# A fused language-model block on one core: two more units of each attention step are written ahead, and SyncE's queue is reordered

## The chip, the cores and the metric

The kernel runs on one core of a Trainium2 chip. The metric is the device time of one execution in microseconds (us). Engines are called PE (TensorE, the matmuls), DVE (VectorE), ACT (ScalarE), POOL (GpSimd) and SP (SyncE, which here only issues DMA transfers).

## What is computed

An embedding with a short grouped convolution and ReLU, then attention with a residual, then a block with layer norms and eight experts chosen by position, all in float32 on 2 sequences of 1024 tokens with 128 channels. The change touches the attention, whose core in the reference is

```python
q, k, v = (proj(Wq), proj(Wk), proj(Wv))          # 8 heads of 64
dots = jnp.einsum('bhqd,bhkd->bhqk', q, k) * scale
attn = jax.nn.softmax(dots, axis=-1)
out = jnp.einsum('bhqk,bhkd->bhqd', attn, v)
out = jnp.einsum('bne,ce->bnc', out, Wo)
```

and at its edges the first layer norms of the block behind it.

## The kernel before

**Steps, units, parts.** There are 8 attention steps (STEPS), one for each sequence and pair of heads. A step has 16 units (s, kc, half): 128 keys (kc 0 to 7) against 512 queries (half 0 or 1) for two heads. A unit is scores on PE into a pair of PSUM banks, exponentials on ACT out of it, and the values' product on PE. Units run in 8 parts of two, half 0 in parts 0 to 3 and half 1 in parts 4 to 7.

**Maxima.** The softmax needs each query's maximum ahead of the exponentials. It is taken from a product of its own ("max" items, matmuls of L576, two heads each), which DVE reduces (L1066), and which runs ahead of the units: 14 items stand in front of step 0 (AHEAD), then two in each part. So the 8 items of half 0 of step s+1 end in part 4 of step s, those of half 1 in part 0 of step s+1. When a half is complete, DVE joins it (L1074), and SP does the rest (max_rows, L426): 8 column transfers bring the maxima from partitions into rows (L438), one stores the rows in HBM (L443), one loads them back spread over 128 partitions as a plane (L448). SP waits between these for each to land.

**Written ahead or not.** A unit in FILLED gets its PSUM banks filled with minus the plane before its scores are added: by ACT alone (fill, L903), or, in HALVED, one head by DVE (fill_half, L1110, a "share") and one by ACT (L901). A unit that is UNFILLED instead gets a fourth pair of matmuls from minus_rows and max_rows_of (in scores, L623 to L638), which needs only the rows. 30 of the 128 units are unfilled: the first two of every step among them (LATE_PLANES), because their banks would have to be filled in the last part of the step before.

**Order.** part_items and beside_values write one list for all engines, and each engine runs its own part of it strictly in order: a waiting instruction holds up all behind it on its engine. k and q of step s+1 are computed in part 0 of step s. Units use banks 0 to 3 (EVEN_PAIR, ODD_PAIR), and "max" items take two each from a ring of three banks (RING), so that each shares a bank with the one before it and must wait until that one's first head has been reduced (holders, release).

**Reciprocals.** The softmax sums of step s-1 go through SP in step s (spread, L412): a transfer to a flat layout, a reciprocal on DVE in part 4, a store to HBM (L417), and two loads of 256 KB that spread it (L422), after which POOL multiplies (normalise, L1293). SP's order in a step is: rows of (s, 1), all of spread, rows of (s+1, 0), in steps 4 to 6 two experts' weights (L454).

**Step 7** has no more k, q and, after part 0, no maxima; instead the first sequence's output product (wo, 64 matmuls of L585), its layer norms on ACT ("norms") and two products for the block behind it (nt, xa) run among its units.

Of the kernel before, what the change touches and what calls it, by code (L numbers as in the profile page):

```python
# [51 lines left out]
AHEAD = 14  # L52
# [75 lines left out]
NO_SLOT = ("join", "hidden", "pv", "o", "inv", "norms", "fill", "share")  # L128
# [26 lines left out]
def step_pairs(items):  # L155

    pairs, turn = [], 0
    for item in items:
        if item[0] == "exp":
            pairs.append(ODD_PAIR if item[2] % 2 else EVEN_PAIR)  # L160
        elif item[0] in ("k", "wo"):
# [45 lines left out]
def build(nc, x, tables, w_in, wo_in, small_in, next_b, fc_in, out):  # L207
    VOCAB = VOCAB_ROWS
    with ExitStack() as ctx:
# [136 lines left out]
        rows_stored, plane_loaded, filled_in, half_filled = (sem(n) for n in ("rows_stored", "plane_loaded", "filled_in", "half_filled"))  # L346
# [57 lines left out]
        def _(sp):  # L404
# [7 lines left out]
            def spread(s):  # L412
# [4 lines left out]
                sp.dma_start(inv_dram[:, :], inv_flat[:, :]).then_inc(inv_stored, 16)  # L417
                sp.wait_ge(inv_stored, s * 16 + 16)
# [7 lines left out]
            def max_rows(v, half):  # L426
# [6 lines left out]
                for c in range(GROUP):  # L433
                    qc = half * GROUP + c
                    if i == 0:
                        sp.wait_ge(max_joined, c + 1)
                    for h in range(2):
                        sp.dma_start(max_rows_of[v % 2][h * D:h * D + 1, qc * CHUNK:(qc + 1) * CHUNK].bitcast(F32),  # L438
                                     maxes[:, h, qc:qc + 1].bitcast(F32)).then_inc(rows_loaded, 16)
                sp.wait_ge(rows_loaded, ROW_COUNT * (i + 1))  # L440
# [4 lines left out]
                if i > 1:  # L445
                    sp.wait_ge(filled_in, filled_up_to(i - 2, FILLED))
                    sp.wait_ge(half_filled, filled_up_to(i - 2, HALVED))
# [37 lines left out]
        def _(pe):  # L485
# [241 lines left out]
            for s in range(STEPS):  # L727
                for item, n in numbered(STEP_ITEMS[s], FIRST[s]):
# [7 lines left out]
                    if item[0] == "exp" and item[1:] in FILLED:  # L736
                        pe.wait_ge(filled_in, FILLED.index(item[1:]) + 1)
                        if item[1:] in HALVED:
                            pe.wait_ge(half_filled, HALVED.index(item[1:]) + 1)
# [46 lines left out]
        def _(act):  # L786
# [80 lines left out]
            def early_norms(which, dst, done):  # L867

                for j in range(KCH):
# [22 lines left out]
            def fill(unit_item):  # L892
# [7 lines left out]
                if unit_item[1:] in HALVED:  # L900
                    act.activation(to[:, 1, :], plane[:, 1, :], ACT.Copy, scale=-1.0).then_inc(filled_in, 1)  # L901
                else:
                    act.activation(to, plane, ACT.Copy, scale=-1.0).then_inc(filled_in, 1)  # L903
# [18 lines left out]
            for s in range(STEPS):  # L922
                for item, n in numbered(STEP_ITEMS[s], FIRST[s]):
                    if item[0] in ("fill", "share") and item[1:] in FILLED:
# [3 lines left out]
                    elif item == ("norms", 1):  # L928
                        ln_sqrt(0)
                    elif item == ("norms", 2):  # L930
                        act.wait_ge(shifted, 2)
                        early_norms(1, normed2, n2_made)
                    elif item == ("norms", 3):
                        early_norms(0, h1n, n1_made)
# [48 lines left out]
        def _(dve):  # L983
# [119 lines left out]
            def fill_half(unit_item):  # L1103
# [48 lines left out]
            def dve_step(s):  # L1152
                for item, n in numbered(STEP_ITEMS[s], FIRST[s]):
                    if item[0] == "inv":
                        invert(item[1])
                    elif item[0] == "share" and item[1:] in HALVED:
                        fill_half(item)
                    elif item[0] == "join":
                        join_last_pair()
                    elif item == ("norms", 1):  # L1160
# [197 lines left out]
```

## Time and profile before

| what | value |
|---|---|
| median of 3 executions | 402.34 us (402.18 to 472.35) |
| the profiled execution | 404.02 us, of which span 402.2 us |
| PE busy | 386.5 us (96%), 2378 matmuls |
| POOL busy | 292.9 us (73%) |
| ACT busy | 290.1 us (72%) |
| DVE busy | 261.8 us (65%) |
| mean granted TensorE clock | 0.996 |
| matmuls from minus_rows | 60 |

The span runs from the first to the last instruction. Start and duration in a timeline are in us from its start. The attention steps take most of it, from about 40 to 352 us; in front are embedding, convolution, norms and projections, behind it the experts. A busy PE isn't PE at its peak: matmuls are pipelined, so the distance between starts tells more than the durations.

### The profile page before, as it was taken

What the parts mean: (1) busy time and instruction counts of PE and PEld (TensorE: products, weight loads), DVE (VectorE), ACT (ScalarE), POOL (GpSimd) and SP (SyncE); (2) the same over time, 40 slices, a digit from 0 to 9 for tenths busy, and PEclk for the clock granted to TensorE, in tenths of its full rate; (3) what the DMA queues carried; (4) which work ended last, traced back from release to release, by engine and by line L of the source; (5) the groups of instructions that cost most, each with busy time, mean ns of one, the idle gap of its engine ahead of it and who ended that gap; (6) DMA issues with size and microseconds to landing.
All of it is one profiled execution on the core that took longest, in us unless ns stands there. A gap on an engine that the chain in (4) does not pass through costs nothing.

```text
span 402.2 us, 6740 instructions
## 1 busy us (share of the span) xinstructions
PE 386.5 (96%) x2378; PEld 221.6 (55%) x2378; DVE 261.8 (65%) x470; ACT 290.1 (72%) x402; POOL 292.9 (73%) x145
## 2 busy tenths in 40 slices
PE   8988899999999999999999999999999887999996
PEld 8754644554464446444544544454457434489995
DVE  6998677676867776766778687767773401664322
ACT  3665489778968886887889688968861897636763
POOL 3170099969899999989998999999897676900021
PEclk9999899999999999999999999999999999999999
DMA  4001010101222022112012420251034105000001
GB/s 141 8 0 53 0 55 0 54 3 52 57 53 54 4 53 54 54 41 66 2 55 55 133 75 4 55 157 56 22 69 125 53 1 155 4 2 15 13 28 52
DMA packets 28229, 19.45 MB, mean 48 GB/s; under 512 B 21249, under 2 KB 23681, under 8 KB 28197
## 3 DMA queue, kind: packets, MB, share of 16 engines
q1 hardware_dynamic: 27620, 18.05, 16.8%
q10 hardware_dynamic: 576, 0.98, 0.8%
q8 instruction: 19, 0.31, 0.4%
q14 instruction: 14, 0.11, 0.1%
HBM read 17.72 MB, written 1.17 MB: 47 GB/s over the span
## 4 chain that ended last, share of the span: by engine, by line
PE 75%; ACT 14%; issue 5%; DVE 4%; ACTq 0%; DVEq 0%
PE psum L649 22%; PE psum L638 20%; ACT probs L834 8%; PE psum L576 8%; PE psum L564 5%; PE psum L585 4%; PE psum L706 4%; PE psum L695 4%; PE psum L540 2%; ACT psum L903 2%; PE psum L660 1%; ACT attn_out L911 1%; PE psum L515 1%; DVE half_maxes L1062 1%; PE psum L601 1%
## 5 line engine op out<-in xcount | busy, mean ns | idle before, releaser
L1066 DVE TENSOR_REDUCE half_maxes<-psum 128x1 f32<-128x512 f32 x228 | 146.5, 684 | 38.1 <-PE psum L576 37.8
L834 ACT ACTIVATE probs<-psum 128x1024 f32<-128x1024 f32 x128 | 128.6, 1018 | 40.7 <-PE psum L638 39.6
L649 PE MATMUL psum<-probs,v_all 128*64 128x512 f32 x512 | 123.7, 604 | 0.0
L1282 POOL TENSOR_TENSOR sums<-sums,probs 128x1024 f32<-128x1024 f32 x31 | 74.2, 2393 | 2.6 <-ACT probs L834 2.5
L1282 POOL TENSOR_TENSOR odd_sum<-odd_sum,probs 128x1024 f32<-128x1024 f32 x31 | 74.4, 2399 | 0.0
L1282 POOL TENSOR_TENSOR sums<-probs 128x1024 f32<-128x1024 f32 x16 | 38.0, 2376 | 44.1 <-ACT probs L834 44.0
L649 PEld LDWEIGHTS psum<-probs,v_all 128*64 128x64 f32 x512 | 31.2, 136 | 62.2 <-issue 47.5
L1110 DVE TENSOR_SCALAR psum<-max_plane 128x512 f32<-128x512 f32 x46 | 32.0, 695 | 45.0 <-ACT probs L834 45.0
L638 PE MATMUL psum<-q_round,k_round 64*128 64x512 f32 x256 | 55.2, 426 | 5.3 <-ACT psum L903 2.0
L576 PE MATMUL psum<-k_round,q_round 64*128 64x512 f32 x256 | 56.5, 445 | 3.1 <-DVE half_maxes L1062 1.5
L903 ACT ACTIVATE psum<-max_plane 128x1024 f32<-128x1024 f32 x52 | 53.6, 1030 | 4.5
L576 PEld LDWEIGHTS psum<-k_round,q_round 64*128 64x128 f32 x256 | 24.0, 185 | 53.5 <-DVE half_maxes L1066 34.9
L638 PE MATMUL psum<-q_round,k_rest 64*128 64x512 f32 x256 | 51.2, 393 | 0.0
L638 PE MATMUL psum<-q_rest,k_round 64*128 64x512 f32 x256 | 51.0, 392 | 0.0
L1288 POOL TENSOR_TENSOR sums<-sums,odd_sum 128x1024 f32<-128x1024 f32 x16 | 38.1, 2382 | 1.3
L638 PEld LDWEIGHTS psum<-q_round,k_round 64*128 64x128 f32 x256 | 24.4, 185 | 26.1 <-ACT psum L903 14.5
L1282 POOL TENSOR_TENSOR odd_sum<-probs 128x1024 f32<-128x1024 f32 x16 | 38.3, 2395 | 0.0
L1310 POOL TENSOR_TENSOR probs<-probs,residual 128x256 f32<-128x256 f32 x7 | 5.1, 726 | 42.7 <-ACT probs L954 42.7
L901 ACT ACTIVATE psum<-max_plane 128x512 f32<-128x512 f32 x46 | 27.7, 602 | 5.2
L638 PEld LDWEIGHTS psum<-q_round,k_rest 64*128 64x128 f32 x256 | 24.5, 185 | 5.5
L638 PEld LDWEIGHTS psum<-q_rest,k_round 64*128 64x128 f32 x256 | 24.5, 186 | 3.2
L947 ACT ACTIVATE probs<-psum,small 128x128 f32<-128x128 f32 x64 | 17.4, 383 | 11.4 <-PE psum L695 11.4
(123 smaller groups left out, 456.4 us busy)
## 6 DMA issues: line engine op xcount, KB each, us to landing
max_plane<-rows_scratch SPq DMA_DIRECT2D x16, 512.0 KB, 3.7
inv_sb<-inv_scratch SPq DMA_DIRECT2D x14, 256.0 KB, 3.9
max_rows_of<-maxes SPq DMA_DIRECT2D x128, 0.5 KB, 2.0
v_all<-in_fc SPq DMA_DIRECT2D x4, 512.0 KB, 5.7
fc_late<-in_fc SPq DMA_DIRECT2D x4, 512.0 KB, 5.8
out_h<-probs SPq DMA_DIRECT2D x8, 128.0 KB, 1.8
v_all<-in_w ACTq DMA_DIRECT2D x3, 256.0 KB, 3.6
woT<-in_wo SPq DMA_DIRECT2D x1, 256.0 KB, 3.5
```

Of the source, the lines that this page charges most:

```text
L564: last = pe.matmul(slot[:, half, :], ws[:, w, v % PAIRS, :], xs[:, cols[half]], start=(i == 0), stop=(i == 2))
L576: last = pe.matmul(slot[:, h, :], q_round[p][head_rows(h), qc * CHUNK:(qc + 1) * CHUNK], k_round[p][head_rows(h), half * BANK:(half + 1) * ...
L638: last = pe.matmul(slot[:, h, :], stationary, qs[head_rows(h), cols], start=(i == 0 and not ahead), stop=(i == len(terms) - 1), skip_group ...
L649: last = pe.matmul(out_bank[head_rows(h), :], v_all[:, s, kc, head_rows(h)], probs[unit(s, kc, half) % TILES][:, h, :], start=(kc == 0), s ...
L834: last = act.activation(probs[u % TILES][:, heads, :], source, ACT.Exp, scale=SCALE)
L901: act.activation(to[:, 1, :], plane[:, 1, :], ACT.Copy, scale=-1.0).then_inc(filled_in, 1)
L903: act.activation(to, plane, ACT.Copy, scale=-1.0).then_inc(filled_in, 1)
L947: act.activation(hidT[d % 2][:, i, r, :], slot[:, i, r], ACT.Gelu, bias=fc1_b_col[:, e * HC + r:e * HC + r + 1]).then_inc(hid_made, 1)
L1066: dve.reduce_max(half_maxes[:, h, qc, keys:keys + 1], slot[:, h, :], AX.X).then_inc(maxed, 1)
L1110: dve.tensor_scalar(pair_view(PAIRS_OF[n])[:, 0, :], plane[:, 0, :], -1.0, None, ALU.mult).then_inc(half_filled, 1)
L1282: pool.tensor_tensor(chain[:, :, :], first[:, :, :], probs[kc][:, :, :], ALU.add).then_inc(own, 1)
L1288: pool.tensor_tensor(even[:, :, :], even[:, :, :], odd_sum[:, :, :], ALU.add).then_inc(own, 1)
```

## The change

- AHEAD goes from 14 to 12; the first five parts of step 0 take 1, 2, 3, 3 and 3 maxima (FIRST_COUNTS), after which the count is what it was. k and q of step 1 move from part 0 to part 1.
- The first two units of steps 1 to 7 are now written ahead, in the last part of the step before (following looks across the step's end): the first shared by DVE and ACT, the second by ACT. In step 0 six units more are unfilled. In all 18 units are unfilled.
- In step 7 twelve units are written wholly by DVE (VECTOR_FILLED); wo moves to the end of part 0 and from the units' banks to the ring; nt moves from part 3 to part 4, xa from 5 to 6, and the norms are cut into four groups of four.
- On SP the former spread and max_rows are cut in two each, and in a step the columns of (s+1, 0) go out in front of the reciprocals' loads.

```diff
-AHEAD = 14
+AHEAD = 12
...
-FFN_ITEMS = {(STEPS - 1, 0): [("wo",)], (STEPS - 1, 3): [("nt",)], (STEPS - 1, 5): [("xa",)], (STEPS - 1, 6): [("last den", 0)]}
-
-
-LATE_PLANES = [(s, kc, 0) for s in range(STEPS) for kc in (0, 1)]
-BEHIND_K, BEHIND_Q = [(s, 2, 0) for s in range(STEPS)], [(s, 3, 0) for s in range(STEPS)]
-UNFILLED = LATE_PLANES + BEHIND_Q + [(0, 2, 0), (STEPS - 1, 2, 0), (STEPS - 1, 4, 0), (STEPS - 1, 5, 0), (STEPS - 1, 0, 1), (STEPS - 1, 1, 1)]
+FFN_ITEMS = {(STEPS - 1, 4): [("nt",)], (STEPS - 1, 6): [("xa",), ("last den", 0)]}
+LAST_NORMS = {1: [("roots",)], 2: [("n2", 0)], 3: [("n2", 1)], 4: [("n1", 0)], 5: [("n1", 1)]}
+
+
+FIRST_UNITS = [(0, kc, 0) for kc in (0, 1)]
+BEHIND_K = [(0, 4, 0)] + [(s, 2, 0) for s in range(1, STEPS - 1)]
+BEHIND_Q = [(0, 5, 0)] + [(s, 3, 0) for s in range(1, STEPS - 1)]
+FIRST_PLANES = [(0, kc, 0) for kc in (2, 3, 6)] + [(0, kc, 1) for kc in (0, 1, 2, 3)]
+UNFILLED = FIRST_UNITS + BEHIND_Q + FIRST_PLANES + [(STEPS - 1, 4, 0), (STEPS - 1, 5, 0)]
...
-HALVED = [u for u in FILLED if u[1] % 2 == 0 and u not in BEHIND_K]
+BESIDE_LAST_MAXES = [(STEPS - 1, kc, 0) for kc in (0, 1)]
+SCALAR_FILLED = [u for u in FILLED if u[0] < STEPS - 1 or u in BESIDE_LAST_MAXES]
+HALVED = [u for u in SCALAR_FILLED if u[1] % 2 == 0 and u not in BEHIND_K]
+VECTOR_FILLED = [u for u in FILLED if u in HALVED or u not in SCALAR_FILLED]
...
-    if part == 0 and s + 1 < STEPS:
+    if part == (0 if s > 0 else 1) and s + 1 < STEPS:
         items += [("k", s + 1), ("q", s + 1)]
...
+FIRST_COUNTS = (1, 2, 3, 3, 3)
+
+
+def maxes_before(turn):
+
+    return AHEAD + sum(FIRST_COUNTS[:turn]) + 2 * max(0, turn - len(FIRST_COUNTS))
+
+
 def part_items(s, part):
 
-    maxes = [("max", *m) for m in MAXES[AHEAD + 2 * (s * PARTS + part):][:2]]
-    items = maxes[:1]
+    turn = s * PARTS + part
+    maxes = [("max", *m) for m in MAXES[maxes_before(turn):maxes_before(turn + 1)]]
     first, second = [("exp", *u) for u in units_of(s, part)]
-    following = units_of(s, part + 1) if part + 1 < PARTS else []
-    items += [first] + [("share", *u) for u in following if u in HALVED] + [second] + maxes[1:]
-    beside = beside_values(s, part)
-    items += beside
-    items += [("fill", *u) for u in following if u in FILLED and u not in HALVED]
-    if s > 0 or part > 0:
-        items += [("pv", *u) for u in units_of(*divmod(s * PARTS + part - 1, PARTS))]
+    following = units_of(*divmod(turn + 1, PARTS)) if turn + 1 < STEPS * PARTS else []
+    shares = [[("share", *u)] * (u in VECTOR_FILLED) for u in following] or [[], []]
+    if turn == 0:
+        items = [first, second] + maxes
+    elif len(maxes) == 3:
+        items = [maxes[0], first] + shares[0] + [maxes[1], second] + shares[1] + maxes[2:]
+    elif (s, part) == (STEPS - 1, 0):
+        items = maxes[:1] + [first, second] + maxes[1:] + shares[0] + shares[1]
+    else:
+        items = maxes[:1] + [first] + shares[0] + [second] + shares[1] + maxes[1:]
+    items += beside_values(s, part)
+    items += [("fill", *u) for u in following if u in SCALAR_FILLED]
+    if turn > 0:
+        items += [("pv", *u) for u in units_of(*divmod(turn - 1, PARTS))]
     if part == 0 and s > 0:
         items.append(("o", s - 1, 1))
     if part == 4:
         items += [("o", s, 0)] + [("inv", s - 1)] * (s > 0)
-    if s == STEPS - 1 and part in (1, 2, 3):
-        items.append(("norms", part))
+    if s == STEPS - 1:
+        items += [("wo",)] * (part == 0) + LAST_NORMS.get(part, [])
     return items
...
-            max_rows(0, 0)
+            load_rows(0, 0)
+            spread_rows(0, 0)
             early, late = list(EARLY_EXPERTS), list(LATE_EXPERTS)
             for s in range(STEPS):
-                max_rows(s, 1)
+                load_rows(s, 1)
+                spread_rows(s, 1)
                 if s > 0:
-                    spread(s - 1)
+                    store_inverse(s - 1)
                 if s + 1 < STEPS:
-                    max_rows(s + 1, 0)
+                    load_rows(s + 1, 0)
+                if s > 0:
+                    spread_inverse(s - 1)
+                if s + 1 < STEPS:
+                    spread_rows(s + 1, 0)
...
-            def fill_half(unit_item):
+            def vector_fill(unit_item):
 
                 _, s, kc, half = unit_item
                 n = ALL_ITEMS.index(("exp", s, kc, half))
-                plane = max_planes[half][:, :].rearrange("p (h n) -> p h n", h=2)
+                to, plane = pair_view(PAIRS_OF[n]), max_planes[half][:, :].rearrange("p (h n) -> p h n", h=2)
                 dve.wait_ge(*release(ALL_ITEMS[holders(n)[0][0]]))
                 dve.wait_ge(plane_loaded, 16 * (2 * s + half) + 16)
-                dve.tensor_scalar(pair_view(PAIRS_OF[n])[:, 0, :], plane[:, 0, :], -1.0, None, ALU.mult).then_inc(half_filled, 1)
+                heads = slice(0, 1 if unit_item[1:] in HALVED else 2)
+                dve.tensor_scalar(to[:, heads, :], plane[:, heads, :], -1.0, None, ALU.mult).then_inc(vector_filled, 1)
```

load_rows is max_rows up to its column transfers, spread_rows the rest of it (from the wait for them, L443 on); store_inverse is spread up to the store of the reciprocals, spread_inverse the rest of it, with the two loads.

## Rows read from the trace of the kernel before

**Rows 1.** Stretches: us, then busy us of each engine, clock, DMA share, GB/s

```profile
core 0: us, PE busy (x) PEld busy (x) DVE busy (x) ACT busy (x) POOL busy (x), PEclk, DMA share, GB/s
151.00:188.00 37.00, 36.87 (x222) 17.81 (x218) 27.01 (x43) 29.84 (x34) 35.29 (x16) 1.00 0.18 44
```

**Rows 2.** Timeline of PE, into step 4: start, duration, what

```profile
186.31 0.40 PE L576 MATMUL psum<-k_round,q_round 64*128 64x512 f32 x2
...
188.51 0.50 PE L576 MATMUL psum<-k_round,q_round 64*128 64x512 f32 x2
...
189.54 0.39 PE L638 MATMUL psum<-max_rows_of,minus_rows 64*128 64x512 f32 x2
189.76 0.39 PE L638 MATMUL psum<-q_round,k_round 64*128 64x512 f32 x2
```

**Rows 3.** Timeline of ACT, same transition; in brackets the idle time before

```profile
185.82 1.94 ACT L834 ACTIVATE probs<-psum 128x1024 f32<-128x1024 f32 x2 [0.40 <-PE psum L638]
189.97 1.96 ACT L834 ACTIVATE probs<-psum 128x1024 f32<-128x1024 f32 x2 [2.21 <-PE psum L638]
```

**Rows 4.** Timeline of DVE, same transition

```profile
176.45 0.17 DVE L1074 TENSOR_REDUCE maxes<-half_maxes 128x8 fp32r<-128x16 f32 x1
...
186.75 1.29 DVE L1066 TENSOR_REDUCE half_maxes<-psum 128x1 f32<-128x512 f32 x2 [0.33 <-PE psum L576]
```

**Rows 5.** Timeline of SP's queue, same transition: when a DMA is issued

```profile
176.81 0.32 SPq L417 DMA_DIRECT2D inv_scratch<-inv_flat  x1
178.21 1.15 SPq L422 DMA_DIRECT2D inv_sb<-inv_scratch  x2
179.45 5.04 SPq L438 DMA_DIRECT2D max_rows_of<-maxes  x8
185.93 0.53 SPq L443 DMA_DIRECT2D rows_scratch<-max_rows_of  x1
187.54 0.32 SPq L448 DMA_DIRECT2D max_plane<-rows_scratch  x1
```

**Rows 6.** Issue to landing: inv_sb's two (178 to 180), first column (179.4 to 180), plane (187 to 189)

```profile
DMA to landing us min/median/max: 3.6/3.9/4.1
...
max_rows_of<-maxes SPq DMA_DIRECT2D x1, 0.5 KB, 3.4
...
max_plane<-rows_scratch SPq DMA_DIRECT2D x1, 512.0 KB, 3.6
```

**Rows 7.** Groups by line, DVE's share: count, then busy, mean ns, idle before

```profile
L1110 DVE TENSOR_SCALAR psum<-max_plane 128x512 f32<-128x512 f32 x46 | 32.0, 695 | 45.0 <-ACT probs L834 45.0
```

**Rows 8.** Issue to landing, plane with experts' loads behind it, 262.2 to 263

```profile
max_plane<-rows_scratch SPq DMA_DIRECT2D x1, 512.0 KB, 4.4
```

**Rows 9.** Timeline of POOL, same transition

```profile
188.17 2.40 POOL L1293 TENSOR_TENSOR attn_out<-attn_out,inv_sb 128x1024 f32<-128x1024 f32 x1
```

**Rows 10.** Stretches around PE's clock, columns as in rows 1

```profile
38.00:41.00 3.00, 1.39 (x12) 0.85 (x10) 3.00 (x3) 0.00 (x0) 0.00 (x0) 1.00 0.46 175
41.00:44.50 3.50, 3.50 (x17) 2.27 (x14) 2.01 (x4) 1.86 (x2) 0.00 (x0) 0.51 0.00 0
332.00:336.00 4.00, 1.71 (x12) 0.72 (x10) 0.85 (x2) 3.77 (x6) 1.74 (x1) 1.00 0.02 2
```

**Rows 11.** PE's waits from 37 to 51 us: in total, times, longest

```profile
PE psum L576 <- ACT q_round L845: 1.2, 1, 1.2
PE psum L576 <- DVE half_maxes L1062: 1.0, 1, 1.0
PE psum L638 <- DVE half_maxes L1062: 0.6, 1, 0.6
```

**Rows 12.** PE's waits from 300 to 352 us

```profile
PE psum L638 <- ACT psum L903: 2.0, 2, 1.0
PE psum L638 <- DVE psum L1110: 1.6, 2, 1.3
PE psum L592 <- ACT normed L870: 1.2, 1, 1.2
PE psum L638 <- DVE residual L1125: 0.8, 1, 0.8
```

More of the change, by code:

```diff
@@ L125, in step_items @@
     return items
-NO_SLOT = ("join", "hidden", "pv", "o", "inv", "norms", "fill", "share")
+NO_SLOT = ("join", "hidden", "pv", "o", "inv", "roots", "n1", "n2", "fill", "share")
 def numbered(items, first):
@@ L160, in step_pairs @@
             pairs.append(ODD_PAIR if item[2] % 2 else EVEN_PAIR)
-        elif item[0] in ("k", "wo"):
+        elif item[0] == "k":
             pairs.append(EVEN_PAIR)
@@ L345, in build @@
         rows_loaded = sem("rows_loaded")
-        rows_stored, plane_loaded, filled_in, half_filled = (sem(n) for n in ("rows_stored", "plane_loaded", "filled_in", "half_filled"))
+        rows_stored, plane_loaded, scalar_filled, vector_filled = (sem(n) for n in ("rows_stored", "plane_loaded", "scalar_filled", "vector_filled"))
         summed = [[sem(f"summed_{p}_{half}") for half in ("low", "high")] for p in ("even", "odd")]
@@ L410, in _, with store_inverse @@
             sp.dma_start(woT[:, :, :], wo_in).then_inc(wo_loaded, 16)
-            def spread(s):
+            def store_inverse(s):
                 sp.wait_ge(den_copied, s + 1)
@@ L417, in spread, with spread_inverse @@
                 sp.dma_start(inv_dram[:, :], inv_flat[:, :]).then_inc(inv_stored, 16)
+            def spread_inverse(s):
                 sp.wait_ge(inv_stored, s * 16 + 16)
@@ L424, in spread, with load_rows @@
                                  .partition_broadcast(D).rearrange("p a n -> p (a n)")).then_inc(inv_loaded, 16)
-            def max_rows(v, half):
+            def load_rows(v, half):
                 i = 2 * v + half
@@ L439, in max_rows, with spread_rows @@
                                      maxes[:, h, qc:qc + 1].bitcast(F32)).then_inc(rows_loaded, 16)
+            def spread_rows(v, half):
+                i = 2 * v + half
                 sp.wait_ge(rows_loaded, ROW_COUNT * (i + 1))
@@ L445, in max_rows @@
                 if i > 1:
-                    sp.wait_ge(filled_in, filled_up_to(i - 2, FILLED))
-                    sp.wait_ge(half_filled, filled_up_to(i - 2, HALVED))
+                    sp.wait_ge(scalar_filled, filled_up_to(i - 2, SCALAR_FILLED))
+                    sp.wait_ge(vector_filled, filled_up_to(i - 2, VECTOR_FILLED))
                 sp.dma_start(max_planes[half][:, :], rows_dram[half:half + 1].rearrange("a h n -> a (h n)").partition_broadcast(128)
@@ L736, in _ @@
                     if item[0] == "exp" and item[1:] in FILLED:
-                        pe.wait_ge(filled_in, FILLED.index(item[1:]) + 1)
-                        if item[1:] in HALVED:
-                            pe.wait_ge(half_filled, HALVED.index(item[1:]) + 1)
+                        if item[1:] in SCALAR_FILLED:
+                            pe.wait_ge(scalar_filled, SCALAR_FILLED.index(item[1:]) + 1)
+                        if item[1:] in VECTOR_FILLED:
+                            pe.wait_ge(vector_filled, VECTOR_FILLED.index(item[1:]) + 1)
                     else:
@@ L865, in ln_sqrt, with early_norms @@
                                bias=eps_squared[:, 0:1]).then_inc(ln_std, 1)
-            def early_norms(which, dst, done):
-                for j in range(KCH):
+            def early_norms(which, half, dst, done):
+                if (which, half) == (1, 0):
+                    act.wait_ge(shifted, 2)
+                for j in range(half * GROUP, (half + 1) * GROUP):
                     act.activation(dst[:, j, :], residual[:, j, :], ACT.Identity, bias=shift[:, which, j:j + 1],
@@ L900, in fill @@
                 if unit_item[1:] in HALVED:
-                    act.activation(to[:, 1, :], plane[:, 1, :], ACT.Copy, scale=-1.0).then_inc(filled_in, 1)
+                    act.activation(to[:, 1, :], plane[:, 1, :], ACT.Copy, scale=-1.0).then_inc(scalar_filled, 1)
                 else:
-                    act.activation(to, plane, ACT.Copy, scale=-1.0).then_inc(filled_in, 1)
+                    act.activation(to, plane, ACT.Copy, scale=-1.0).then_inc(scalar_filled, 1)
             def o_copy(s, half):
@@ L923, in _ @@
                 for item, n in numbered(STEP_ITEMS[s], FIRST[s]):
-                    if item[0] in ("fill", "share") and item[1:] in FILLED:
+                    if item[0] == "fill":
                         fill(item)
@@ L927, in _ @@
                         o_copy(item[1], item[2])
-                    elif item == ("norms", 1):
+                    elif item[0] == "roots":
                         ln_sqrt(0)
[L930 to L934, printed above, removed]
+                    elif item[0] == "n2":
+                        early_norms(1, item[1], normed2, n2_made)
+                    elif item[0] == "n1":
+                        early_norms(0, item[1], h1n, n1_made)
                     if n is not None:
@@ L1155, in dve_step @@
                         invert(item[1])
-                    elif item[0] == "share" and item[1:] in HALVED:
-                        fill_half(item)
+                    elif item[0] == "share":
+                        vector_fill(item)
                     elif item[0] == "join":
                         join_last_pair()
-                    elif item == ("norms", 1):
+                    elif item[0] == "roots":
                         ln_inverse(0)
```

## The prediction

> **What bounds the kernel now.** I read the page's list of engines first, then the table of stretches, then the timelines of one transition between two attention steps, engine by engine, SP's queue last. In a step of 37.0 us TensorE (PE) is busy 36.87 us and shows a granted clock of 1.00, GpSimd 35.29, ScalarE 29.84, VectorE 27.01 [rows 1]. So PE sets the pace, and any time in which PE has nothing to do is lost whole: nothing else stands ahead of it. GpSimd's 35.3 us would be the next floor, far enough off for the sizes below. The thing to see in PE's timeline is that part 7 of a step and part 0 of the next run on without a gap: max product at 186.31, then the values' products, then the next max product at 188.51 [rows 2].
>
> **The change, part by part.**
>
> *Products saved on PE.* A unit that isn't written ahead needs one more pair of matmuls (minus_rows). The pair starts at 189.54 and the next one at 189.76 [rows 2]: about 0.23 us a pair with the neighbours' spacing. Before, 30 of 128 units have it; after, 18: the two first units of steps 1 to 7 are gained (14), four more in step 7 too, and six of step 0 are given up: 14 + 4 - 6 = 12. Sum: -12 x 0.23 = **-2.8 us**, about 0.46 us for each transition.
>
> *What writes them instead.* In part 7 ScalarE writes 1.5 units and VectorE half a unit more. Counted as work this costs nothing: ScalarE is idle 2.21 us before the exponentials at 189.97 [rows 3] and VectorE has 10 us spare in a step [rows 1]. But these instructions wait, and what matters is for what.
>
> *When the plane of maxima is there.* These are the times of the transition into step 4. The last half maximum of the half is joined at 176.45 + 0.17 = 176.62 [rows 4]. SP issues the reciprocals' store at 176.81, their two loads at 178.21, the eight columns from 179.45 to 184.49, the rows' store at 185.93 (1.44 after the last issue) and the plane at 187.54 (1.61 later) [rows 5]. The plane lands 3.6 us later, 191.1 [rows 6]. With the columns in front, they are issued from about 177.2 to 182.25 and the reciprocals' loads from 182.3 to 183.5. The last column has landed at 183.7, and the rows' store goes out then. From here there are two ends:
> - nothing in its way: plane issued 183.7 + 1.6 = 185.3, landed **188.9**;
> - the store stands in the queue behind the two loads of 256 KB. Rows 6 show such a case: the first column, issued at 179.45 right behind those loads, took 3.4 us (landed 182.85) and not the 2.0 or so of one with nothing ahead (0.63 of issue plus 1.44). The second load, issued about 178.8, lands 3.6 to 4.1 later, so at 182.4 to 182.9: the small transfer came when the large one had. In the new order the second load goes out at 182.9 and lands 186.5 to 187.0; the store with it; the plane then lands at **190.1 to 190.6**.
>
> I take the second. The Trainium skill (DMA: Bandwidth & Descriptors, section Queues, rings and completion order) says that an engine takes descriptors in ring order but that a later one may finish its write first; the 3.4 us agree with its first half, and by its second half alone the sum would be that of the first end.
>
> *Who waits.* VectorE's share of unit (s+1, 0, 0) stands in part 7 behind the first exponential, which starts at 185.82 and has ended by about 186.9 [rows 3]. The plane is 2 us late at the one end and 3.2 to 3.7 at the other. VectorE runs in program order, so the reductions of part 7's second max product, done at 186.75 before [rows 4], now stand behind that share. The next max product of PE (188.51) shares a bank with that product and waits until its first head is reduced. After the plane: a share of 0.695 [rows 7], a first reduction of 0.65 (half of 1.29 [rows 4]), some 0.1 between engines: 1.45 us. PE resumes at 190.35 at the one end, at 191.55 to 192.05 at the other, instead of 188.51. PE waits **1.8** or **3.0 to 3.5 us**; I take 3.3. Behind it stand the scores, k and q of the next step and all values' products. Six transitions (into steps 2 to 7) have reciprocals: 6 x 3.3 = **+19.8 us**. Into steps 5, 6 and 7 the experts' loads are issued right behind the plane, and such a plane took 4.4 us, not 3.6 [rows 8]: 3 x 0.8 = **+2.4 us**. Into step 1 there are no reciprocals, and parts 4 and 5 of step 0 have no units that VectorE writes ahead while PE has two more pairs in each; I take 0, with 1.2 us (the 1.8 less about 0.55 for the reciprocals' store) as the bound above.
>
> *What waits for the reciprocals.* Their loads land at about 187.0, 4 us later than before. GpSimd normalises at 188.17 [rows 9]: hidden by 1.1 us, and PE's wait adds to that. If it weren't, GpSimd would wait, and only after that the exponentials.
>
> *The clock.* From 38 to 41 us PE was busy 1.39 of 3.0 us, and from 41.0 to 44.5 its clock was granted at 0.51, the 1.2 GHz level instead of 2.4. A stretch with 1.71 of 4.0 busy (332 to 336) was not followed by a drop [rows 10]. A single wait of 3.3 us is longer than any there. I take one such slow stretch for each of the six: 3.4 us at half speed lose 1.7: 6 x 1.7 = **+10.2 us**; the bound below is 0. The Trainium skill (TensorE: Matmul & The Clock Gate, Part 1) has the clock fall with low activity and return with work, which these rows agree with.
>
> *Start.* AHEAD = 12 takes two maxima off the front, and k and q of step 1 go into part 1. PE's waits of 1.0 and 0.6 us before the first exponential and of 1.2 us on q_round [rows 11] go, since PE then has exponentials and values' products to run, and the slow stretch of rows 10 (1.7 us) should go with them: 1.0 + 0.6 + 1.2 + 1.7 = **-4.5 us**. Three maxima a part are 3 x 1.29 of reductions plus at most one share, about what PE needs for such a part; bound: nothing gained.
>
> *Step 7.* PE waits 2.0 + 1.6 + 1.2 + 0.8 = 5.6 us there [rows 12]. The 0.8 (units waiting for the wo bank) goes; VectorE writes 12 whole units (up to 1.39 us each, twice 0.695), ScalarE loses that work, and its 16 norms come in fours. But roots and both table loads still stand between exponentials while PE has no more than two units of lead. I take **-1.0 us**, bounds -4 and +2.
>
> *Sum.* -2.8 + 19.8 + 2.4 + 10.2 - 4.5 - 1.0 = +24.1. The profiled execution took 404.0 us (span 402.2), the median is 402.34, its span's size; on it: **426 us**, 6% slower.
>
> **The rivals.**
> - *The clock holds.* All as above, without the +10.2: 416 us. For it: no drop after 332 to 336. Against it: there PE worked between two short waits.
> - *The store isn't held by the loads.* The wait is 1.8, not 3.3: 9 us less. If the clock holds as well: 402.3 - 2.8 + 10.8 + 2.4 - 4.5 - 1.0 = 407 us; if it drops, 417. For it: the store is 4 KB and needs only its own rings; against it: the 3.4 us of rows 6.
> - *The plane is in time* (the other side). The columns go 2.25 us earlier, and if the rest of the chain closes up so that the plane lands before the share asks for it (186.9), no wait arises: 402.3 - 2.8 - 4.5 - 1.0 = 394 us. This decides from a landing 4.2 us before today's 191.1; the lead of the columns is 2.25. Between 186.9 and there every us late is a us of PE in each of six steps; break-even is a wait of about 0.9 us, a landing near 188.
> - *Nearly no change.* The landing is somewhat earlier than my lower end, or the gains at the start and in step 7 reach their bounds: 396 to 409 us.
>
> **How the numbers follow.** Forecast (queue holds the store, clock drops: 420 to 434): 0.50. Clock holds (411 to 420): 0.22. Store not held: 0.15, half near 407, half near 417. In time: 0.06. Nearly no change: 0.07. The likeliest gives 426. A measurement of this kernel tells about 2% from no change: below 394.3 faster (0.06), above 410.4 slower (0.50 + 0.22 + 0.07 = 0.79), between them same (0.08 + 0.07 = 0.15). The range reaches from the store not held with the clock holding, 407, rounded to 408, to 433, the forecast with waits of 3.7 us and a smaller gain at the start; about 0.2 lies outside.
>
> **What would show it.** In the new profile: 18 x 2 matmuls from minus_rows instead of 60. In SP's timeline the columns' issue ahead of the reciprocals' loads, and the gap from the last column's issue to the plane's issue growing from 3.05 us to about 4.7 (queue holds) or staying (not). On PE six waits of about 3.3 us on half_maxes, once a step, in front of part 0's max product, with VectorE idle before its share until a DMA lands. A clock below 1.00 once behind each. Wrong would be: no such waits, or a plane landed by the end of part 7's first exponential; waits of half the size with the gap unchanged, the second rival; waits in place with a clock of 1.00, the first. Waits of the step-7 kind instead would say that the fills, not the plane, are late.

## The result

| | before | after |
|---|---|---|
| median | 402.31 us | 430.18 us (429.15 to 431.09) |
| ratio | | 1.069, 95% interval 1.066 to 1.072 |
| span of the profiled execution | 402.2 us | 429.3 us |
| mean granted clock | 0.996 | 0.964 |
| matmuls from minus_rows | 60 | 36 |

One execution of before took 472 us, and the ratio leaves it out. The change made the kernel 6.9% slower; 426 us was forecast.

PE's waits by what ended them (in total, times, longest) in the kernel after:

```profile
PE psum L610 <- DVE half_maxes L1102: 31.1, 9, 5.6
PE psum L672 <- DVE psum L1147: 2.2, 4, 1.0
```

Of the 31.1 us, seven waits stand at the start of a step: 1.33, 5.26, 3.69, 3.73, 4.79, 5.62 and 5.60 into steps 1 to 7, 30.0 together. Before there was no such wait: PE went on at 188.51 without idle time [rows 2]. The transition into step 4 in the kernel after, SP's queue first (start, duration of the issue):

```profile
185.97 0.32 SPq L438 DMA_DIRECT2D inv_scratch<-inv_flat  x1
186.39 5.01 SPq L462 DMA_DIRECT2D max_rows_of<-maxes  x8
191.49 1.19 SPq L446 DMA_DIRECT2D inv_sb<-inv_scratch  x2
192.86 0.52 SPq L471 DMA_DIRECT2D rows_scratch<-max_rows_of  x1
195.88 0.32 SPq L476 DMA_DIRECT2D max_plane<-rows_scratch  x1
```

The columns are out at 191.40 and landed by 192.86, but from the rows' store to the plane's issue it takes 3.02 us, against 1.61 before [rows 5]: the store came back late, behind the reciprocals' two loads. The plane then took this long from issue to landing:

```profile
DMA to landing us min/median/max: 3.5/3.5/3.5
```

So it landed at 199.4. DVE's timeline (in brackets the idle time and what ended it):

```profile
193.69 1.29 DVE L1102 TENSOR_REDUCE half_maxes<-psum 128x1 f32<-128x512 f32 x2 [0.28 <-PE psum L610]
199.42 0.69 DVE L1147 TENSOR_SCALAR psum<-max_plane 128x512 f32<-128x512 f32 x1 [4.45 <-DMA max_plane<-rows_scratch]
200.03 2.65 DVE L1102 TENSOR_REDUCE half_maxes<-psum 128x1 f32<-128x512 f32 x4
```

DVE stands idle 4.45 us before its share, and the two reductions of a max product that PE had started at 194.87 begin only at 200.03, where before they ran at 186.75, right behind their product [rows 4]. PE's timeline ends the chain:

```profile
195.18 1.94 PE L683 MATMUL psum<-probs,v_all 128*64 128x512 f32 x8
200.85 0.50 PE L610 MATMUL psum<-k_round,q_round 64*128 64x512 f32 x2 [3.73 <-DVE half_maxes L1102]
...
201.96 0.67 PE L672 MATMUL psum<-q_round,k_round 64*128 64x512 f32 x2
202.39 0.67 PE L672 MATMUL psum<-q_rest,k_round 64*128 64x512 f32 x2
```

The second pair of lines is the clock: starts 0.43 us apart and not 0.23. The same stretch in the table of windows (us, PE busy, weight loads, DVE, ACT, POOL, clock, DMA share, GB/s):

```profile
197.00:207.00 10.00, 6.27 (x29) 4.79 (x28) 4.63 (x8) 4.47 (x5) 9.41 (x5) 0.83 0.14 49
```

**Where the 27.1 us between the spans arose.** PE's first product of step 1 stood at 77.27 us before and at 77.08 after: -0.2, although a wait of 1.3 us is in it. From there to the same product of step 7 it took 222.5 us (to 299.74) and now 252.0 (to 329.11): +29.6. Step 7, up to its last sums' product (353.76 and 380.86), took 54.0 and now 51.7: -2.3. The rest, 48.4 us, is the same. -0.2 + 29.6 - 2.3 = 27.1.

### The profile page after: what moved, and what is told of

It is laid out like the page before. It is cut to its first block, busy times and chain, and to the rows that moved or that the text cites. A ratio compares the mean times of both kernels' runs of the same rounds, so it can differ in the third digit from the quotient of the medians.

```text
span 429.3 us, 6704 instructions
## 1 busy us (share of the span) xinstructions
PE 389.0 (91%) x2354; PEld 229.6 (53%) x2354; DVE 274.7 (64%) x483; ACT 284.5 (66%) x402; POOL 292.3 (68%) x145
## 4 chain that ended last, share of the span: by engine, by line
PE 61%; DMA 15%; DVE 9%; SPq 8%; issue 4%; ACT 4%; DVEq 0%
PE psum L683 15%; PE psum L672 14%; SPq L462 7%; PE psum L610 7%; DMA max_plane<-rows_scratch 6%; PE psum L598 5%; DMA rows_scratch<-max_rows_of 5%; DMA max_rows_of<-maxes 4%; PE psum L619 3%; PE psum L740 3%; PE psum L729 3%; DVE half_maxes L1102 3%; ACT probs L869 2%; PE psum L574 2%; DVE psum L1147 2%
## 5 line engine op out<-in xcount | busy, mean ns | idle before, releaser
L1102 DVE TENSOR_REDUCE half_maxes<-psum 128x1 f32<-128x512 f32 x232 | 148.9, 683 | 32.9 <-PE psum L610 31.9
L869 ACT ACTIVATE probs<-psum 128x1024 f32<-128x1024 f32 x128 | 125.3, 1022 | 58.6 <-PE psum L672 58.1
L610 PE MATMUL psum<-k_round,q_round 64*128 64x512 f32 x256 | 59.6, 464 | 32.0 <-DVE half_maxes L1102 31.1
L1147 DVE TENSOR_SCALAR psum<-max_plane 128x512 f32<-128x512 f32 (+1 forms) x57 | 45.4, 806 | 61.5 <-DMA max_plane<-rows_scratch 35.1
L610 PEld LDWEIGHTS psum<-k_round,q_round 64*128 64x128 f32 x256 | 25.7, 193 | 84.3 <-DVE half_maxes L1102 71.7
L672 PE MATMUL psum<-q_round,k_rest 64*128 64x512 f32 x256 | 53.6, 410 | 0.0
L672 PE MATMUL psum<-q_rest,k_round 64*128 64x512 f32 x256 | 53.3, 408 | 0.0
L672 PEld LDWEIGHTS psum<-q_round,k_round 64*128 64x128 f32 x256 | 25.9, 194 | 11.9 <-DVE psum L1147 6.5
L672 PEld LDWEIGHTS psum<-q_round,k_rest 64*128 64x128 f32 x256 | 26.1, 195 | 5.6
L672 PEld LDWEIGHTS psum<-q_rest,k_round 64*128 64x128 f32 x256 | 26.1, 196 | 4.8
```

Source lines behind the costliest of these rows:

```text
L610: last = pe.matmul(slot[:, h, :], q_round[p][head_rows(h), qc * CHUNK:(qc + 1) * CHUNK], k_round[p][head_rows(h), half * BANK:(half + 1) * ...
L672: last = pe.matmul(slot[:, h, :], stationary, qs[head_rows(h), cols], start=(i == 0 and not ahead), stop=(i == len(terms) - 1), skip_group ...
L869: last = act.activation(probs[u % TILES][:, heads, :], source, ACT.Exp, scale=SCALE)
L1102: dve.reduce_max(half_maxes[:, h, qc, keys:keys + 1], slot[:, h, :], AX.X).then_inc(maxed, 1)
L1147: dve.tensor_scalar(to[:, heads, :], plane[:, heads, :], -1.0, None, ALU.mult).then_inc(vector_filled, 1)
```

## The experiments

The theory: the plane of half 0 isn't there when DVE's share of the next step's first unit asks for it, the share holds the reductions behind it, these hold PE, and the clock drops in the wait. The rivals: the fills cost as work, or SP's new order costs by itself.

**First two units unfilled again.**

```diff
-UNFILLED = FIRST_UNITS + BEHIND_Q + FIRST_PLANES + [(STEPS - 1, 4, 0), (STEPS - 1, 5, 0)]
+UNFILLED = FIRST_UNITS + BEHIND_Q + FIRST_PLANES + [(STEPS - 1, 4, 0), (STEPS - 1, 5, 0)] + [(s, kc, 0) for s in range(1, STEPS) for kc in (0, 1)]
```

> The kernel after, but the first two units of steps 1 to 7 are not written ahead again (14 pairs of matmuls from minus_rows more); all else, SP's order too, as after. Theory (the share that waits for the plane costs PE its waits and the clock drops behind them): the seven waits on half_maxes (30.0 us in the profile after) and the slow stretches (about 12.7 us lost) go, 14 x 0.23 = 3.2 us come back: 430.2 - 30.0 - 12.7 + 3.2 = 391 us. Rival (SP's new order or the new order of fills is what costs): stays above 410 us.

Measured: 392.5 us, ratio to before 0.976 (0.974 to 0.977), clock 1.00; of the waits on half_maxes 1.1 us are left. The whole loss hangs on these 14 units. And all the rest of the change is worth 10 us, far more than I had forecast for it. A step took 36.17 us where it had taken 37.04 (from one k_rest on DVE to the next: 152.92 to 189.09, and 156.79 to 193.83 before), with as many unfilled units. That wanted an explanation of its own (below).

**SP's order of before, with the two units written ahead.**

```diff
+                if s > 0:
+                    spread_inverse(s - 1)
                 if s + 1 < STEPS:
                     load_rows(s + 1, 0)
-                if s > 0:
-                    spread_inverse(s - 1)
-                if s + 1 < STEPS:
                     spread_rows(s + 1, 0)
```

> The kernel after, but SP issues the reciprocals' loads ahead of the columns again, as before. From the reciprocals' store to the plane's issue it was 10.73 us before (176.81 to 187.54) and 9.91 after (185.97 to 195.88). Theory (each us by which the plane lands later is a us of PE in each of six transitions): 430.2 + 6 x 0.8 = 435 us, waits of about 4.5 us. Rival (the reorder gave its full 2.25 us of lead): 430.2 + 13 = 443 us. Rival (it gave nothing): 430 us.

Measured: 439.5 us (ratio 1.092), waits on half_maxes 37.5 in all against 31.1. The reorder did help the change, by 9.3 us in the medians and 7.1 in the two profiled executions (spans 436.4 and 429.3). 6.4 of the 7.1 are waits, the rest a little more slow clock (0.957 against 0.964). Of the 6.4, 0.7 lies in the wait into step 1 (2.08 us instead of 1.33), where there are no reciprocals. From part 7's last max product to the next step's first, the six other transitions lost 5.7 us, 0.95 each: near the 0.8 of my theory, and 1.3 short of the columns' whole lead of 2.25. About that much (1.4) the store behind the loads takes back, as the next experiment shows.

**The reciprocals' loads behind the plane.**

```diff
                 if s + 1 < STEPS:
                     load_rows(s + 1, 0)
+                    spread_rows(s + 1, 0)
                 if s > 0:
                     spread_inverse(s - 1)
-                if s + 1 < STEPS:
-                    spread_rows(s + 1, 0)
```

> The kernel after, but the reciprocals' loads are issued behind the plane, so that nothing large stands between the columns and the rows' store. Theory (the store is held in the queue by the two loads: 3.0 us from its issue to the plane's issue after, 1.6 before): the gap returns to 1.6, the reciprocals' two issues (1.2 us) no longer delay it either, the waits fall by about 1.5 us each, six times 9 us: about 421 us, less if the clock then drops less often; the reciprocals come later, at about GpSimd's turn. Rival (the store is slow for another reason): gap stays near 3.0, 430 us.

Measured: 419.9 us, 10.3 less than after (9.6 by the two profiled spans). SP's queue into step 4:

```profile
183.85 5.01 SPq L462 DMA_DIRECT2D max_rows_of<-maxes  x8
190.30 0.53 SPq L471 DMA_DIRECT2D rows_scratch<-max_rows_of  x1
191.91 0.32 SPq L476 DMA_DIRECT2D max_plane<-rows_scratch  x1
192.32 1.15 SPq L446 DMA_DIRECT2D inv_sb<-inv_scratch  x2
```

From store to plane 1.61 us again. A store of 4 KB came back 1.4 us later with 512 KB ahead of it in its queue. Whether their order in the queue did that, or only that they were under way at the same time, the runs don't separate. All waits on half_maxes came to 24.6 us, 6.5 less. GpSimd, whose reciprocals now come later, cost nothing that can be seen.

**Matmuls in the wait.**

```diff
+                        if s > 0 and item == ("max", *MAXES[min(maxes_before(s * PARTS), len(MAXES) - 1)]):
+                            m, k = holders(n)[0]
+                            pe.wait_ge(*release(ALL_ITEMS[m], k))
+                            p, cols = item[1] % 2, slice(item[2] * CHUNK, (item[2] + 1) * CHUNK)
+                            for _ in range(14):
+                                pe.matmul(bank(PAIRS_OF[n][0]), q_round[p][:, cols], k_round[p][:, 0:BANK], start=True, stop=True)
                         for m, k in holders(n):
                             pe.wait_ge(*release(ALL_ITEMS[m], k))
```

> The kernel after, with 14 matmuls of 512 columns (3.0 us) whose result is overwritten put into PE's waits at the start of steps 1 to 7, on a bank that is free by then. Theory (the granted clock falls because PE has nothing to do in the wait, and that loses about 12.7 us beside the waits): clock 1.00 or near, 430.2 - 12.7 = 417.5 us, into step 1 up to 1.7 us longer. Rival (the drop costs nothing, since the others wait for PE anyway or it comes from something else): 430 us.

Measured: 423.3 us, 6.9 less than after. The window that showed 0.83 above:

```profile
197.00:207.00 10.00, 9.15 (x48) 6.38 (x48) 5.78 (x9) 5.33 (x6) 9.12 (x4) 1.00 0.14 48
```

The drop does come from PE's idle time. What it costs is best read on stretches that hold no transition, from a step's first max product to the second one of its part 7. In this kernel they are 33.7 to 33.8 us in all six steps. In after they were 33.71 us in step 1, which has no slow stretch, and 35.65, 34.97, 34.96, 34.93 and 35.60 in steps 2 to 6: 7.3 us more. Step 7, from its first product to its last sums' product, took 49.1 us here and 51.75 in after: 2.65 more. So the six drops cost 10.0 us.

The median fell by less, 6.9 (8.3 between the profiled spans). Into step 1, where the wait had been only 1.3, the matmuls delayed PE by 2.0 us: from part 7's last max product to the next first it took 5.61 us instead of 3.60. My 12.7, half of all slow time in which PE worked, was too much: even at full clock, k's first matmul waits about 0.3 us for an exponential in these places, and a slow PE covers that.

**The fills' order on ScalarE.** The gain of 0.87 us a step wasn't in my prediction. In the diff, ACT handles only "fill" items, and "fill" items now include the shared units; before, ACT wrote its head of a shared unit at the "share" item, between the two exponentials of a part. This is that edit alone, on the kernel before:

```diff
-    items += [("fill", *u) for u in following if u in FILLED and u not in HALVED]
+    items += [("fill", *u) for u in following if u in FILLED]
...
-                    if item[0] in ("fill", "share") and item[1:] in FILLED:
+                    if item[0] == "fill":
```

> The kernel before, with one edit: ScalarE writes its head of a shared unit behind both exponentials of the part, as the kernel after does, not between them. In the first experiment a step took 36.18 us between two k_rest on VectorE, against 37.05 before, with as many unfilled units per step. Theory (ScalarE's fill between the exponentials delayed the second one, and that was the 0.2 to 0.3 us by which parts 3, 5 and 6 were longer): 402.3 - 7 x 0.87 = 396 us. Rival (the shorter step comes from something else, such as where k and q or the reciprocals stand): 402 us.

Measured: 395.5 us, ratio 0.982 (0.979 to 0.984): by itself it makes the kernel before 1.6 to 2.1% faster, clear of the noise. ACT's timeline before, and then in this kernel:

```profile
160.22 1.03 ACT L834 ACTIVATE probs<-psum 128x1024 f32<-128x1024 f32 x1 [0.54 <-PE psum L638]
161.36 0.60 ACT L901 ACTIVATE psum<-max_plane 128x512 f32<-128x512 f32 x1
161.89 1.00 ACT L834 ACTIVATE probs<-psum 128x1024 f32<-128x1024 f32 x1
163.01 1.03 ACT L903 ACTIVATE psum<-max_plane 128x1024 f32<-128x1024 f32 x1
```

```profile
160.08 1.94 ACT L834 ACTIVATE probs<-psum 128x1024 f32<-128x1024 f32 x2 [0.77 <-PE psum L638]
161.90 0.61 ACT L901 ACTIVATE psum<-max_plane 128x512 f32<-128x512 f32 x1
162.42 1.03 ACT L903 ACTIVATE psum<-max_plane 128x1024 f32<-128x1024 f32 x1
163.99 1.94 ACT L834 ACTIVATE probs<-psum 128x1024 f32<-128x1024 f32 x2 [0.54 <-PE psum L638]
```

Two exponentials at a stretch take 1.94 us; with a fill between them it was 2.67 from the first start to the second end (160.22 to 162.89). ACT still comes round in time: it even idles 0.54 before the next part. PE's weight loads show what had waited. Over two steps (118.33 to 192.46 us), before and then in this kernel:

```profile
PEld psum L638 <- ACT psum L903: 3.4, 10, 0.5
```

```profile
PEld psum L638 <- ACT psum L903: 0.3, 2, 0.2
```

With the second exponential late, ACT's whole fill (L903) behind it was late too, and the next scores' weight loads waited for it: 3.1 us less in two steps, and the two steps became 1.7 us shorter.

**First experiment with SP's old order.** The edit of the second experiment on the first one.

> The first experiment (after, first two units unfilled) with SP's order of before. Theory (the queue's order matters only through the plane, and without the two units the plane has more than 4 us of room): same as the first experiment, 392.5 us. Rival (the reorder helps or harms on its own, by later reciprocals or collisions): more than 1 us off it.

Measured: 392.2 us, ratio 0.973 (0.971 to 0.975), the same. The queue's order is worth nothing where nobody asks for the plane in part 7. Of the kernels that leave nothing out this is the fastest, with the first experiment beside it.

**Share behind both reductions.**

```diff
+    elif part == PARTS - 1:
+        items = maxes[:1] + [first, second] + maxes[1:] + shares[0] + shares[1]
     else:
         items = maxes[:1] + [first] + shares[0] + [second] + shares[1] + maxes[1:]
```

> The kernel after, but in part 7 VectorE takes its share of the next step's first unit behind both reductions. Theory (PE's next max product waits for a reduction that is queued behind the share): that product runs at once, and PE waits for the plane plus a share (0.8) before the scores and not for the plane plus share plus half a reduction (1.45) before the max product (0.34): 1.0 us less a transition, seven times: 430.2 - 7 = 423 us; the wait on PE is then on psum L1147 or L940 and not on half_maxes. Rival (the order on VectorE doesn't matter, ScalarE's fills behind the plane are what PE waits for): 430 us.

Measured: 422.5 us. The wait moved to where the theory put it:

```profile
PE psum L674 <- ACT psum L940: 22.8, 7, 4.8
```

Seven waits for ScalarE's fill, 22.8 us, instead of 30.0 us in seven on half_maxes. The order on DVE was a part of the cost, 1 us a transition; the late plane is the rest.

**Maxima one part earlier.** Meant to bring the plane in time:

```diff
-FIRST_COUNTS = (1, 2, 3, 3, 3)
+COUNTS = [1, 2, 3, 3, 3, 2, 2, 2] + [2, 3, 3, 2, 2, 2, 2, 2] + [0, 3, 3, 2, 2, 2, 2, 2] * 5
...
-    return AHEAD + sum(FIRST_COUNTS[:turn]) + 2 * max(0, turn - len(FIRST_COUNTS))
+    return AHEAD + sum(COUNTS[:turn])
...
+                if s + 1 < STEPS:
+                    load_rows(s + 1, 0)
+                    spread_rows(s + 1, 0)
                 if s > 0:
                     store_inverse(s - 1)
-                if s + 1 < STEPS:
-                    load_rows(s + 1, 0)
-                if s > 0:
                     spread_inverse(s - 1)
-                if s + 1 < STEPS:
-                    spread_rows(s + 1, 0)
```

> The kernel after, but from step 1 on the maxima of half 0 are complete at the end of part 3 and not in part 4 (0, 3, 3, 2, 2, 2, 2, 2 a part), and SP handles rows and plane of (s+1, 0) whole ahead of the reciprocals. Theory (the two units gain their 0.46 us a step once the plane is there in time): join to landing 11.7 us against 13.6 from the end of part 3 to the share: no waits into steps 2 to 7, clock 1.00, against the first experiment 14 x 0.23 = 3.2 us less, 1.3 us of wait into step 1 and up to 2 us for two parts of three reductions a step: 390 to 392 us. Rival (the units written ahead cost in their own right, by ScalarE's and VectorE's work): above 396 us.

Measured: 463.5 us (ratio 1.152). A miss by my own edit. Two of its waits:

```profile
DVE inv_flat L1150 <- DMA den_flat<-den_sb: 39.7, 6, 7.1
PE psum L608 <- DVE half_maxes L1100: 53.1, 27, 6.4
```

store_inverse also holds the flat transfer of the sums, and behind the plane's chain it came 6 to 7 us after DVE's reciprocal in part 4 had begun to wait for it: the change's own fault once more, a DVE instruction in front of the reductions that waits for a late transfer. Besides, each part with three maxima made PE wait 1.0 to 1.1 us, over 2 us a step for a gain below 0.5, so that the form as such couldn't pay. It doesn't tell what an early plane is worth. A mended form was not tried.

**The two units from a plane that is there.** In fill and vector_fill:

```diff
-                act.wait_ge(plane_loaded, 16 * (2 * s + half) + 16)
-                to, plane = pair_view(PAIRS_OF[n]), max_planes[half][:, :].rearrange("p (h n) -> p h n", h=2)
+                early = half == 0 and kc < 2 and s > 0
+                act.wait_ge(plane_loaded, 16 * (2 * s + half) + 16 * (not early))
+                to, plane = pair_view(PAIRS_OF[n]), max_planes[1 if early else half][:, :].rearrange("p (h n) -> p h n", h=2)
```

and on SP the load of the next plane of half 1 waits for these reads too.

> The kernel after, but the first two units of steps 1 to 7 are filled from the plane that is already there, that of the step before's half 1, instead of their own. It leaves out the right maxima for these units (the numbers of the output change, the work doesn't): same instructions, same transfers, only nobody waits for the late plane. Theory (the two units are worth their 14 x 0.23 = 3.2 us, and all of the loss is the wait and the clock behind it): the first experiment's 392.5 - 3.2 = 389.3 us, clock 1.00. Rival (ScalarE's and VectorE's work for the two units costs by itself): 392 us or more.

Measured: 390.4 us, clock 1.00. With the same instructions and transfers and no wait, the kernel is 40 us faster than after. The two profiled spans differ by 40.8 us, and the waits and the clock close that: from part 7's last max product to the next first it takes 30.5 us less in the seven transitions, the slow stretches of after cost 9.9 us, and 0.4 arose before part 7 of step 0 ended. Against the first experiment (392.5) the 14 units gain 2.1 us, not 3.2: a step takes 35.95 us, 0.22 less. The pair costs PE 0.23 each, but k's first matmul then waits for the second exponential:

```profile
PE psum L599 <- ACT probs L870: 1.8, 6, 0.3
```

**Both means against the wait.** Share behind the reductions as above, and on SP:

```diff
                 if s > 0:
-                    store_inverse(s - 1)
+                    flatten(s - 1)
                 if s + 1 < STEPS:
                     load_rows(s + 1, 0)
+                    spread_rows(s + 1, 0)
                 if s > 0:
+                    store_inverse(s - 1)
                     spread_inverse(s - 1)
-                if s + 1 < STEPS:
-                    spread_rows(s + 1, 0)
```

where flatten is the flat transfer of the sums alone.

> The kernel after with both means against the wait: on SP only the flat transfer of the sums stays ahead, then columns, store and plane, and the reciprocals' store and loads behind them; on VectorE the share behind both reductions. With the plane ahead of the loads the six waits were 3.0 to 4.5 (mean 3.6), the share behind the reductions took 1.0 off, the reciprocals' store out of the way takes 0.55 (0.42 of issue and the wait for the reciprocal): mean 2.1 us. Theory (each us of wait is a us of the kernel, on the 389.3 us of an early plane): 389.3 + 6 x 2.1 + 0.7 = 403 us if the clock holds, up to 1.4 a transition more if it drops: 411 us. It stays above the first experiment's 392.5 in any case. Rival (the waits overlap with the rest once they are short): near 390 us.

Measured: 405.0 us (401.4 to 406.8), ratio 1.005 (1.002 to 1.008). In the profiled execution (span 402.3) the waits were 10.1 us in seven:

```profile
PE psum L677 <- ACT psum L943: 10.1, 7, 2.5
```

They were 1.0 us into step 1, then 2.2, 0.9, 0.7, 1.3, 1.6 and 2.5: 1.5 in the mean of the six, shorter than my 2.1. The clock fell once, behind the 2.2 us into step 2:

```profile
116.00:119.40 3.40, 3.40 (x16) 2.21 (x14) 1.61 (x4) 2.26 (x3) 0.00 (x0) 0.52 0.64 154
```

Together with 388.5 us, the span of the kernel with the stale plane, 388.5 + 10.1 = 398.6. Of the other 3.7 us, about 1.2 is that slow stretch, and nearly 0.3 more than its wait stands in each of the seven transitions. The execution with the clock at 1.000 took 401.4 us; in the nine others it was 0.985 to 0.996, and they took 404.1 to 406.8. So the order of SP and DVE brings the change back to the time of before, and leaves it 13 us behind the first experiment. What an early plane with the right maxima gives was never measured.

## Why the prediction was right, and where it was off

- **The mechanism** held in every link: columns early, store held, plane late, share in front of the reductions, PE waiting, clock falling. The kernels with the loads behind the plane, the share behind the reductions, the matmuls in the wait and the stale plane show the links one by one.
- **When the plane is there.** From the last column's issue to the plane's 4.7 us were foreseen and 4.5 came. The end with the store held by the loads was the right one, as rows 6 had said; the Trainium skill (DMA: Bandwidth & Descriptors, section Queues, rings and completion order) has it that an engine takes descriptors in ring order, and the 3.02 and 1.61 us agree with that.
- **The waits, 19.8 + 2.4 = 22.2 us, were mis-sized: 30.0.** Where nothing else came in, 3.3 was near (3.69 and 3.73). The three with experts' loads behind the plane took 4.8 to 5.6, not 4.1, and the one into step 2 took 5.3: there the two loads' issue lasted 2.48 us on SP, not 1.18. I had taken one transition's queue for all. Into step 1, the wait was near the bound I gave (1.2) and not 0. And part of it is demand: with ACT's new order parts 5 to 7 are faster, so PE arrives about 0.55 us earlier (11.15 us from the reciprocals' store to the wait, 11.70 before).
- **The clock, 10.2 us,** came to 10.0, partly by luck: I priced six stretches of 3.4 us at 1.7 each, but three of them (into steps 3 to 5) cost 1.2 each, and the other three lasted 6.8 us and cost 1.9, 1.9 and 2.65. The rival that the clock holds fell. The wait of 1.3 us into step 1 was followed by no drop.
- **The saved pairs, -2.8,** came in part: the 14 new units gave 2.1 of their 3.2 us, with k's waits for the exponential (1.8 us in six) against them.
- **The start, -4.5,** failed in one term. The waits and the slow stretch did go, but parts of three maxima last 5.05 us (values' products at 46.41, 51.49, 56.54 and 61.59), not the 4.5 of PE's work: I called three reductions and a share "about what PE needs", and DVE is longer. With the six pairs more (1.4), -3.1 was foreseen and -1.5 came. Even that was the clock: the slow stretch of rows 10, my 1.7, is missing in about two of three executions of before. Those at a clock of 1.00 take 402.3 us, those at 0.996 about 403.7, and the median of 402.3, on which I put the sum, has the time of the first kind. The profiled one (404.0) is of the second. So 1.7 us were taken off a time that didn't hold them; without that the same sum gives 428 us. The kernel that differs from before only in ACT's order has the old start and, in the profiled execution, no drop:

```profile
38.00:41.00 3.00, 1.44 (x10) 0.98 (x10) 3.00 (x3) 0.00 (x0) 0.00 (x0) 1.00 0.41 156
41.00:44.50 3.50, 3.50 (x21) 2.61 (x19) 2.74 (x6) 2.26 (x3) 0.00 (x0) 1.00 0.00 0
```

  Its step 1 begins at 74.79 us, and that of the first experiment, with the new start, at 75.21. The new start gained nothing.
- **Step 7, -1.0:** 54.0 to 51.7 us although the sixth slow stretch lies in it: PE came from its first product to wo in 6.57 us where the kernel with the stale plane took 3.92, so 2.65 lost. Without that it gained 4.9, against 2.4 foreseen (the 1.0 and 1.4 for its six pairs, the first two units' among them): PE's waits there came down to 2.2 us from 5.6 [rows 12], and 0.6 is ACT's order, since with that edit alone step 7 took 53.4.
- **What the prediction didn't have:** ACT's order of fills, 0.87 us in each of seven steps. I read the diff's line in ACT's loop as a new name, and PE's 36.87 busy us of 37.0 as proof that nothing stood ahead of PE. That didn't hold: with ACT's order alone changed, a step of the same work took 36.2 us. It hid in the sum, because waits too small by 7.8 us were offset by about 6 us of gain I didn't see. A total that comes true isn't the proof of its terms.

## What to carry to other kernels

Work written ahead on an in-order engine is only worth its price if its input has landed by then: count back from the place where the instruction stands, not from where its result is needed, and list what is queued behind it. A transfer on which a chain waits is better issued ahead of a large one of the same queue, however small it is; here that was worth 10 us. SP's order was worth nothing where nobody waited for the plane. And when several edits come together, time each alone: here one that the title didn't name made the kernel 1.8% faster by itself, and the two units written ahead took it from 392.5 to 430.2 us, 9.6% slower.

## What the runs showed that was not expected

- Fills of 0.6 us between two exponentials cost 0.87 us a step on ScalarE though that engine was busy for less than 30 of 37 us [rows 1]: they stood on the way from scores to fill to the next scores.
- A clock drop cost less than half of the slow time: 1.2 us for stretches of 3.4 us at 0.50, and 1.9 to 2.65 for those of 6.8, part of them idle or covering other waits.
- The length of a wait alone doesn't tell whether the clock falls behind it. The 2.08 us into step 1 with SP's order of before and the 2.2 us into step 2 of the last kernel were followed by a drop. The 3.00 us into step 3 with the reciprocals' loads behind the plane, and the last kernel's 2.5 us into step 7, were not.
- One kernel can take several times by whether the clock drops in an execution. Before took 402.3 or 403.7 us, and the last kernel 401.4 to 406.8. Kernels whose clock stayed at 0.998 or above lay within 1 us each.
